# Work moved from VectorE to ScalarE and to DMA in a fused anisotropic-diffusion and ternary-convolution kernel

## The chip, the cores and the metric

One core of one Trainium2 chip runs the whole program. The metric is the device time of one execution in microseconds (us); the table below has the median of three runs. The engines are TensorE (PE, matmuls and transposes into PSUM), VectorE (DVE), ScalarE (ACT), GpSimd (POOL, here memsets and the issue of DMAs that add to their destination) and SyncE (SP, here only the issue of DMAs). Each engine runs its own instructions in order; semaphores tie them together.

## The reference

The input x is 8 x 32 x 32 x 64 (batch, row, column, channel), fp32. Cut to what matters:

```python
s = gn(x)                                   # 32 groups of 2 channels, over rows, columns and group
g, g1 = relu(bn(dwconv3x3(s, wg))), relu(bn(dwconv3x3(s, wg1)))
gy, gx = sobel(s)                           # reflecting border
Dx, Dy = 1 / (gy*gy/4 + 1), 1 / (gx*gx/4 + 1)
ux = 0.5 * (roll(g, 1, column) - roll(g, -1, column))
vy = 0.5 * (roll(g1, 1, channel) - roll(g1, -1, channel))
Bx, By, E = 0.2*Dx, 0.2*Dy, 0.2*(ux + vy)
D = 1 / (1 + 2*Bx + 2*By)
h = h0 = s
for _ in range(5):
    prev = h
    h = D * ((1 - 2*Bx - 2*By)*h0 - 2*E*h + (2*Bx - 0.2*g)*roll(h, 1, column) + (2*Bx + 0.2*g)*roll(h, -1, column)
             + (2*By - 0.2*g1)*roll(h, 1, channel) + (2*By + 0.2*g1)*roll(h, -1, channel)) + 0.4*D*s
    h0 = prev
x = x + relu(bn(h))
W3 = alpha * ternary(W)                     # 3 x 3 x 64 x 64, alpha a mean over the kept weights
return x + relu(conv3x3(gn(x), W3) + b)
```

## The kernel before

**Layout.** The batch of 8 is cut in two tiles t of four images. A tile has image row and image on the 128 partitions and 32 columns x 64 channels = 2048 fp32 numbers (1 MB in all) in each; a pass over a tile is thus 128x2048. `coef[:, t, i]` are seven such planes for each tile, `state[:, t, k]` two planes with a border, `ring` three planes. PSUM is used as four slots of 128x1024; `job_table()` gives each PE result (`gy_0_0` is Sobel y, tile 0, half 0) its slot, and PE waits until the slot's former result was read. The order on each engine is written out by hand. `wait_job` waits for a result of PE, `wait_reader` for the engine that reads it.

**First stage, both tiles.** DVE sums x by group, PE averages over partitions, DVE subtracts (`centre`), ACT squares (`square_of`), DVE sums, PE averages (`var_t`), and the inverse root is made by ACT (`rsqrt_first`: Ln, Exp) and one Newton step on DVE (`rsqrt`). `scale_grouped(t)` (L706, DVE) writes the scaled tile in the channel order that the depthwise convolution wants, `scale_s(t)` (L713, DVE) scales it in place. `split_hi` (L718) rounds it to fp32r, `split_lo` (L721) makes the remainder. PE transposes the grouped form (`t2`), applies the Sobel matrices to high and low part (`gy`, `gx`), and runs both depthwise convolutions (`cv_t_0` to `cv_t_3`, L1109 and L1114, with taps that ACT has scaled in `scale_taps`). ACT squares the Sobel results into planes 0 and 1 and brings the convolutions back (`to_natural`).

**Second stage.** `shifted(t)` adds a constant to plane 1 (DVE for tile 0, L789; ACT for tile 1), `denominator(t)` multiplies (DVE), `reciprocal_first(t)` is Ln and Exp on ACT, `newton(t)` two DVE passes. `across_rows` and `across_columns` make planes 4 and 5, `both_diffusivities(t)` (L819, DVE) their sum in plane 2. From it ACT makes D-related planes (`d_of`, `a0_of`), DVE the tap planes (`over_rows`, `over_channels`), and POOL issues DMAs that add the opposite taps (`other_rows`, `other_channels`, `first_source`). The divergence of tile 0 is made by DVE and additive DMAs, with `minus_g` from ACT; that of tile 1 by PE (`divergence`, L1145), for which all `cv_1` must have been read.

**Ring.** A step (k, t) is five or six DVE products of a coefficient plane and a shifted state (L897) into three ring planes; PE transposes and sums them in PSUM (L1155), ACT takes them out, PE turns them back (L1062). `ORDER` interleaves the tiles.

**Tail.** For each tile: `residual` adds x (DVE) and takes statistics, PE averages (`mean2_t`, `var2_t`), `spread` and `second_norm` (DVE, with `rsqrt_first` on ACT) give scale and shift, `normalise` writes eight 64x512 pieces with a step of four numbers (ACT three, DVE five), `upper_half` (ACT) and `lower_half` (DVE) split the result, PE runs the 3x3 convolution (`dense`, L1233) and ACT its ReLU (`relu_dense`), DVE adds (`output_sum`), PE turns the result (`out_natural`), ACT takes it out (`take_out`) and SP stores it. Tile 0 has two such parts, tile 1 four.

## Time and profile before

| | us |
|---|---|
| median of 3 runs | 284.3 (283.94 to 284.4) |
| the profiled execution | 284.37 |
| its span, first to last instruction | 282.6 |
| VectorE busy | 251.6 |
| TensorE busy | 235.3 |
| ScalarE busy | 130.0 |
| first ring product on VectorE starts | 92.97 |

The span is 1.8 us shorter than the time, since the start and the end of an execution lie outside it. An engine that is busy for most of the span need not be what sets the end; that is read from what each waits for. In a timeline row, the brackets behind a group say how long the engine idled ahead of it and what ended that.

### The profile page before, as it was taken

To read this page: it belongs to the slowest core of one execution; us is meant where nothing else is said; L and a number is where in the kernel's file an instruction comes from. 1 tells how busy PE (TensorE), PEld (TensorE's weight loads), DVE (VectorE), ACT (ScalarE), POOL (GpSimd) and SP (SyncE) were. 2 spreads that over 40 slices of the span, in tenths; PEclk is the share of its full clock that TensorE was granted. 3 is DMA by queue.
4 is the path that set the end of the run, shared out by engine and by line. 5 is a ranking of instruction groups with operands and counts; after the bars stand their busy time and mean duration, and the time that the engine had idled before them with its cause. 6 is when DMAs were issued, how large, how long until landed. Compare 5 with 4: busy or idle time off the path is not lost.

```text
span 282.6 us, 5201 instructions
## 1 busy us (share of the span) xinstructions
PE 235.3 (83%) x2264; PEld 210.7 (75%) x2264; DVE 251.6 (89%) x199; ACT 130.0 (46%) x202; POOL 15.9 (6%) x35
## 2 busy tenths in 40 slices
PE   0137999999759998279999999999999876699793
PEld 0136899889725597279999999898989776688682
DVE  3899999999999979999999999999999978986820
ACT  3295678876973204602723516061420515336743
POOL 2000000003300101111000101010101000000000
PEclk9999999999968999959999999999999999979999
DMA  7950000007992701990700425176700040000123
GB/s 201 345 118 0 0 6 3 2 0 148 205 207 43 148 0 37 203 204 3 151 0 2 93 58 111 39 174 125 148 3 1 0 147 3 2 0 0 45 106 148
DMA packets 6758, 22.84 MB, mean 81 GB/s; under 512 B 2768, under 2 KB 3024, under 8 KB 4944
## 3 DMA queue, kind: packets, MB, share of 16 engines
q0 software_dynamic: 2160, 13.63, 24.2%
q1 hardware_dynamic: 4432, 8.56, 9.9%
q8 instruction: 18, 0.29, 0.4%
q10 hardware_dynamic: 144, 0.33, 0.4%
q14 instruction: 4, 0.03, 0.0%
HBM read 6.79 MB, written 2.10 MB: 31 GB/s over the span
## 4 chain that ended last, share of the span: by engine, by line
DVE 49%; PE 36%; issue 8%; ACT 4%; DMA 1%; DVEq 0%; ACTq 0%
DVE ring L897 22%; PE psum L1155 16%; DVE coef L637 8%; PE psum L1233 7%; PE psum L1145 7%; PE psum L1062 3%; DVE first_two L980 3%; DVE coef L940 2%; PE psum L1092 2%; ACT coef L370 2%; DVE lo_s L721 2%; DVE state L713 2%; DVE ring L706 1%; DMA bn<-in_norms 1%; DVE hi_s L718 1%
## 5 line engine op out<-in xcount | busy, mean ns | idle before, releaser
L897 DVE TENSOR_TENSOR ring<-coef,state 128x2048 f32<-128x2048 f32 x51 | 113.4, 2286 | 2.7 <-PE psum L1155 2.5
L1155 PE MATMUL psum<-mats,ring 128*128 128x128 f32 x816 | 97.7, 280 | 13.8 <-DVE ring L897 13.8
L1155 PEld LDWEIGHTS psum<-mats,ring 128*128 128x128 f32 x816 | 92.5, 145 | 17.2 <-DVE ring L897 16.7
L370 ACT ACTIVATE state<-psum 128x1024 f32<-128x1024 f32 x36 | 35.1, 1029 | 83.9 <-PE psum L1155 70.1
L637 DVE SCALAR_TENSOR_TENSOR coef<-coef 128x2048 f32<-128x2048 f32 x16 | 36.6, 2290 | 0.5
L1114 PEld LDWEIGHTS psum<-coef,state 32*128 32x128 f32 x672 | 19.4, 187 | 1.7 <-issue 1.7
L1114 PE MATMUL psum<-coef,state 32*128 32x64 f32 x672 | 20.1, 271 | 0.2 <-issue 0.2
L1233 PE MATMUL psum<-hi,dense_m 128*128 128x512 f32 x48 | 20.0, 417 | 0.0
L370 ACT ACTIVATE coef<-psum 128x512 f32<-128x512 f32 (+1 forms) x22 | 17.3, 791 | 5.7 <-PE psum L1092 4.3
L1233 PE MATMUL psum<-lo,dense_m 128*128 128x512 f32 x48 | 19.3, 403 | 0.0
L1155 PE MATMUL psum<-mats,first_two 128*128 128x128 f32 x144 | 17.2, 273 | 1.2 <-ACT state L370 1.2
L370 ACT ACTIVATE coef<-coef 128x2048 f32<-128x2048 f32 (+1 forms) x10 | 17.6, 1779 | 0.2
L1155 PEld LDWEIGHTS psum<-mats,first_two 128*128 128x128 f32 x144 | 16.0, 141 | 1.4 <-ACT state L370 1.4
L1062 PE MATMUL psum<-mats,state 128*128 128x128 f32 x128 | 15.4, 273 | 0.7 <-ACT state L370 0.7
L1062 PEld LDWEIGHTS psum<-mats,state 128*128 128x128 f32 x128 | 14.1, 141 | 1.2 <-ACT state L370 1.1
L1145 PE MATMUL psum<-coef,mats 128*128 128x512 f32 (+2 forms) x20 | 9.8, 632 | 4.6 <-ACT first_two L370 4.6
L951 DVE TENSOR_TENSOR coef<-coef 128x512 f32<-128x512 f32 (+1 forms) x6 | 5.2, 870 | 8.3 <-ACT coef L370 8.3
L1092 PE MATMUL psum<-lo_s,sobel_m 128*128 128x512 f32 (+2 forms) x48 | 11.4, 372 | 0.5 <-DVE lo_s L721 0.5
L1092 PE MATMUL psum<-hi_s,sobel_m 128*128 128x512 f32 (+2 forms) x48 | 11.3, 372 | 0.5 <-DVE hi_s L718 0.5
L980 DVE TENSOR_TENSOR first_two<-coef,state 128x2048 f32<-128x2048 f32 x5 | 11.4, 2285 | 0.0
L1246 PE MATMUL psum<-gsum,mats 128*128 128x32 f32 x4 | 1.2, 404 | 12.1 <-DVE gsum L671 12.1
L370 ACT ACTIVATE coef<-psum,outp,wred 128x512 f32<-128x512 f32 (+1 forms) x6 | 5.5, 918 | 11.9 <-PE psum L1233 11.9
(132 smaller groups left out, 277.3 us busy)
## 6 DMA issues: line engine op xcount, KB each, us to landing
first_two<-coef POOLq DMA_DIRECT2D x7, 1024.0 KB, 7.3
coef<-coef POOLq DMA_DIRECT2D x4, 1024.0 KB, 9.0
coef<-in_x SPq DMA_DIRECT2D x2, 1024.0 KB, 7.2
coef<-in_wide_taps SPq DMA_DIRECT2D x3, 384.0 KB, 8.0
ring<-in_x SPq DMA_DIRECT2D x2, 512.0 KB, 6.1
ring<-in_x SPq DMA_DIRECT2D x1, 1024.0 KB, 11.2
out<-coef SPq DMA_DIRECT2D x2, 512.0 KB, 3.1
out<-coef SPq DMA_DIRECT2D x4, 256.0 KB, 2.4
```

Source lines behind the costliest of these rows:

```text
L370: return nc.scalar.activation(dst, src, func, **kw)
L637: return V.scalar_tensor_tensor(out=out_ap, in0=in0, scalar=scalar, in1=in1, op0=op0, op1=op1)
L713: signal(V.tensor_tensor(s, s, root(t).unsqueeze(1).broadcast_to([128, W, C]), ALU.mult), s_ready, t + 1)
L721: V.tensor_tensor(wc(s_parts[1][:, :]), h_at(t, 0), wc(s_parts[0][:, :].bitcast(f32)), ALU.subtract)\
L897: V.tensor_tensor(wc(ring[:, slot, :]), wc(coef[:, t, a, :]), h_at(t, k, dw, dc), ALU.mult)\
L980: V.tensor_tensor(wc(first_two[t][:, :]), wc(coef[:, t, A0, :]), h_at(t, k), ALU.mult)\
L1062: ins = nc.tensor.transpose(dst[:, j * 128:j * 128 + 128], src, ident)
L1092: ins = mm(dst[:, bank * BANK + to * C:bank * BANK + (to + count) * C], sobel_m[:, m, :], part[:, frm * C:(frm + count) * C], start=(i == ...
L1114: ins = mm(banks[a][:, j * 2 * W:(j + 1) * 2 * W], sT[t][p, 8 * h + j, dy * BT:dy * BT + 128], taps(8 * h + j)[p, dy, :, :].rearrange("p v ...
L1145: ins = mm(out_ap, m, src, start=(i == 0), stop=(i == len(pieces) - 1), skip_group_check=True)
L1155: ins = mm(slot_ap(name)[:, (j % 8) * 128:(j % 8) * 128 + 128], src[:, j * 128:j * 128 + 128], ident, is_transpose=True, start=first and j ...
L1233: ins = mm(to, dense_m[:, b, dy, :], rows[:, j0 + b:j0 + b + 4, dy * BT:dy * BT + 128], start=(n == 0), stop=(n == len(steps) - 1))
```

## The change

- Tile 0's rounding (`split_hi(0)`), tile 0's shifted square (`shifted(0)`) and tile 1's grouped order (`reorder(1)`, a copy of the already scaled tile in place of `scale_grouped(1)`) are made by ACT. DVE's `scale_s(1)` comes right behind its root, `split_hi(1)` and `denominator(0)` behind that. The ternary weights are made in three pieces instead of two.
- ACT scales the taps of groups 5 to 12 in one go ahead of `split_hi(0)`; `square_of(1)` comes ahead of the transposes' copies. PE runs both high passes of the y Sobel of tile 0 ahead of both low ones, and `var_1` ahead of the x Sobel.
- On ACT `d_of(0)` comes ahead of the second Sobel square of tile 1, `minus_g` behind it, and the copies into `dense_m` ahead of `reciprocal_first(1)`.
- `both_diffusivities(1)` is replaced by two DMAs: SP copies plane 4 into plane 2 once `across_rows(1)` is done, POOL adds plane 5. `d_of(1)` waits for them.
- In the tail, `group_mean2(0)` moves ahead of the source's transposes of step (4, 1), `group_var2(0)` one product forward, the asking for the root is a step of its own behind the first product, and ACT normalises six of tile 0's eight pieces. `group_mean2(1)` and `group_var2(1)` move into `dense(0, 0)`, behind matmuls 18 and 22 of 24. Tile 1's output is cut in 512, 512, 512, 256 and 256 columns instead of four times 512.

On ACT, the rows ahead of tile 0's reciprocal (`coef<-coef,minus`): the squares of the Sobel results are `coef<-psum 128x1024`. Before:

```order
L370 ACTIVATE coef<-psum 128x1024 [waits pe_job] x3
L370 ACTIVATE rs_ln<-rs_in 128x32 [waits rs_asked]
L370 ACTIVATE rs_y<-rs_ln 128x32 [waits act_step]
L370 ACTIVATE coef<-psum 128x1024 [waits pe_job]
...
L370 ACTIVATE last_taps<-last_taps,scales 128x3x32 [waits taps_in4]
L370 ACTIVATE last_taps<-last_taps,scales 128x3x32
L370 ACTIVATE coef<-coef,minus 128x2048 [waits den_const,u_ready]
```

And now, with the shift and the grouped copy between the last square and the reciprocal:

```order
L380 ACTIVATE coef<-psum 128x1024 [waits pe_job] x2
L380 ACTIVATE coef<-coef 128x2048 [waits slot_free0,slot_free3]
L380 ACTIVATE ring<-state 128x128x8x2 [waits s_ready]
L380 ACTIVATE coef<-coef,minus 128x2048 [waits den_const,u_ready]
L380 ACTIVATE coef<-coef 128x2048 [waits act_step]
```

Two full passes stand where the remaining taps stood, and the taps moved forward.

On ACT, from the copy of -g (`state<-coef`) to the first `to_natural` of tile 1; `d_of(0)` is the row that waits for sb_ready. Before:

```order
L370 ACTIVATE state<-coef 128x2048 [waits slot_free0,slot_free1,slot_free3,slot_free2]
L370 ACTIVATE coef<-psum 128x1024 [waits pe_job] x3
L370 ACTIVATE coef<-coef 128x2048 [waits sb_ready]
L370 ACTIVATE coef<-psum 128x1024 [waits pe_job]
L370 ACTIVATE coef<-coef 128x2048 [waits slot_free3,slot_free2]
L370 ACTIVATE coef<-coef 128x2048
L370 ACTIVATE coef<-coef,minus 128x2048 [waits den_const,u_ready]
```

And now:

```order
L380 ACTIVATE coef<-psum 128x1024 [waits pe_job]
L380 ACTIVATE coef<-coef 128x2048 [waits sb_ready]
L380 ACTIVATE coef<-psum 128x1024 [waits pe_job]
L380 ACTIVATE state<-coef 128x2048 [waits slot_free0,slot_free1,slot_free3,slot_free2]
L380 ACTIVATE coef<-psum 128x1024 [waits pe_job] x2
L380 ACTIVATE coef<-coef 128x2048 [waits slot_free3,slot_free2]
L380 ACTIVATE coef<-coef 128x2048
L380 ACTIVATE dense_m<-ring 64x3x64 [waits zero_ready,tern_ready]
```

`d_of(0)` moved from behind the third square to behind the first, `minus_g` from ahead of all to the middle.

On DVE, the rows from the root of tile 1 to `newton(0)` (the row that waits for y_ready). Before:

```order
L706 TENSOR_TENSOR ring<-state,gsum 128x128x8x2 [waits xm_ready,dve_step]
L789 TENSOR_SCALAR coef<-coef 128x2048 [waits slot_free0,slot_free3]
L637 SCALAR_TENSOR_TENSOR coef<-coef 128x2048 [waits shifted_ready,slot_free2,slot_free1]
L713 TENSOR_TENSOR state<-state,gsum 128x32x64 [waits s_grouped_ready,u_ready]
L718 CAST hi_s<-state 128x2048 [waits pe_job,s_ready]
L721 TENSOR_TENSOR lo_s<-state,hi_s 128x2048 [waits s_hi]
L637 SCALAR_TENSOR_TENSOR coef<-coef 128x2048 [waits y_ready]
```

And now:

```order
L747 TENSOR_TENSOR state<-state,gsum 128x32x64 [waits xm_ready,dve_step]
L751 CAST hi_s<-state 128x2048 [waits pe_job,s_ready]
L668 SCALAR_TENSOR_TENSOR coef<-coef 128x2048 [waits shifted_ready,slot_free2,slot_free1]
L755 TENSOR_TENSOR lo_s<-state,hi_s 128x2048 [waits s_hi,u_ready]
L814 TENSOR_SCALAR coef<-coef,wred 128x576
L668 SCALAR_TENSOR_TENSOR ring<-coef,wred 128x576 [waits dve_step]
L668 SCALAR_TENSOR_TENSOR coef<-coef 128x2048 [waits y_ready,tern_ready]
```

The first two rows are gone, and the denominator stands behind the scaling and the rounding of tile 1.

The diff, cut to its core:

```diff
+        act_pieces = (((1, 0), (1, 1), (1, 2), (1, 3), (0, 0), (0, 1)), ((1, 0), (1, 1), (1, 2)))
+        dve_pieces = (((0, 2), (0, 3)), ((0, 0), (0, 1), (0, 2), (0, 3), (1, 3)))
+        out_cuts = ((0, HALF, N), (0, BANK, 2 * BANK, 3 * BANK, 3 * BANK + BANK // 2, N))
...
+            sp.wait_ge(row_part, 2)
+            sp.dma_start(coef[:, 1, 2, :], coef[:, 1, 4, :]).then_inc(sb_begun, 16)
...
             other_channels(0)
+            pool.wait_ge(sb_begun, 16)
+            pool.wait_ge(column_part, 2)
+            pool.dma_start(coef[:, 1, 2, :], coef[:, 1, 5, :], accum_op=ALU.add).then_inc(sb_added, 16)
             first_source(0)
...
+            def split_hi(t):
+                act.wait_ge(s_ready, t + 1)
+                copy(wc(s_parts[0][:, :]), h_at(t, 0)).then_inc(s_hi, 1)
+            def shifted(t):
+                for h in range(2):
+                    wait_reader(act, f"gx_{t}_{h}")
+                copy(coef[:, t, 2, :], coef[:, t, 1, :], bias=(1.0 + 2 * DT) * S).then_inc(shifted_ready, 1)
+            def reorder(t):
+                act.wait_ge(s_ready, t + 1)
+                copy(s_grouped[t].rearrange("p (g a w e) -> p a w g e", e=2, a=CP, w=W),
+                     h_at(t, 0).rearrange("p w (a g e) -> p a w g e", a=CP, e=2)).then_inc(s_grouped_ready, 1)
...
-            step(STEPS - 1, 1, ((-1, lambda: spread(0)), (1, lambda: second_norm(0)), (3, lambda: normalise(0))))
+            step(STEPS - 1, 1, ((-1, lambda: spread(0)), (0, lambda: ask_norm(0)), (1, lambda: second_norm(0)),
+                                  (3, lambda: normalise(0))))
...
+                if (k, t) == ORDER[-1]:
+                    group_mean2(0)
                 take_sums(t, k)
                 add_source(t, k)
...
-            dense(0, 0)
+            dense(0, 0, 0, 18)
             group_mean2(1)
-            dense(0, 1, 0, 4)
+            dense(0, 0, 18, 22)
             group_var2(1)
-            dense(0, 1, 4)
+            dense(0, 0, 22)
+            dense(0, 1)
```

## Rows read from the trace of the kernel before

**Rows 1.** the page's busy time of each engine: us, share of the span, instructions

```profile
PE 235.3 (83%) x2264; PEld 210.7 (75%) x2264; DVE 251.6 (89%) x199; ACT 130.0 (46%) x202; POOL 15.9 (6%) x35
```

**Rows 2.** timeline of DVE, 24 to 110: start, us, line, operation, shapes, count

```profile
24.69 1.23 DVE L718 CAST hi_s<-state 128x2048 fp32r<-128x2048 f32 x1
...
37.88 2.29 DVE L706 TENSOR_TENSOR ring<-state,gsum 128x2048 f32<-128x2048 f32 x1
40.09 1.22 DVE L789 TENSOR_SCALAR coef<-coef 128x2048 f32<-128x2048 f32 x1
...
49.57 9.27 DVE L637 SCALAR_TENSOR_TENSOR coef<-coef 128x2048 f32<-128x2048 f32 x4
...
84.77 2.29 DVE L819 TENSOR_TENSOR coef<-coef 128x2048 f32<-128x2048 f32 x1
...
92.97 6.70 DVE L897 TENSOR_TENSOR ring<-coef,state 128x2048 f32<-128x2048 f32 x3
...
101.49 4.49 DVE L897 TENSOR_TENSOR ring<-coef,state 128x2048 f32<-128x2048 f32 x2 [1.82 <-PE psum L1155]
```

**Rows 3.** timeline of ACT, 37 to 83

```profile
37.48 1.02 ACT L370 ACTIVATE coef<-psum 128x1024 f32<-128x1024 f32 x1 [0.98 <-PE psum L1092]
...
43.77 2.01 ACT L370 ACTIVATE coef<-coef,minus 128x2048 f32<-128x2048 f32 x1 [2.09 <-DVE coef L637]
...
76.69 2.02 ACT L370 ACTIVATE dense_m<-ring 64x192 fp32r<-64x192 f32 x6
...
80.83 1.91 ACT L370 ACTIVATE first_two<-state 128x2048 f32<-128x2048 f32 x1
```

**Rows 4.** timeline of PE, 62 to 105

```profile
62.54 1.11 PE L1109 MATMUL psum<-shift_rows,ones_r 128*128 128x512 f32 x4
...
74.81 1.60 PE L1114 MATMUL psum<-last_taps,state 32*128 32x64 f32 x46
81.06 3.86 PE L1145 MATMUL psum<-coef,mats 128*128 128x512 f32 x6 [4.64 <-ACT first_two L370]
...
91.61 1.96 PE L1145 MATMUL psum<-coef,mats 128*128 128x512 f32 x4
...
99.44 5.44 PE L1155 MATMUL psum<-mats,ring 128*128 128x128 f32 x48
```

**Rows 5.** stretches on PE: us, busy, granted clock, DMA share, GB/s

```profile
80.00:84.00 4.00, 2.94 (x4) 0.50 1.05 199
...
244.00:248.00 4.00, 2.02 (x14) 0.88 0.00 0
```

**Rows 6.** groups of instructions on ACT, shapes apart

```profile
L370 ACT ACTIVATE coef<-coef,gn 64x512 f32<-64x512 f32 x6 | 7.4, 1308 | 1.8 <-DVE gn L637 1.8
```

**Rows 7.** the page's DMA issues: KB of each, median us to landing

```profile
coef<-coef POOLq DMA_DIRECT2D x4, 1024.0 KB, 9.0
coef<-in_x SPq DMA_DIRECT2D x2, 1024.0 KB, 7.2
```

**Rows 8.** timeline of DVE, 228 to 262

```profile
228.63 0.17 DVE L637 SCALAR_TENSOR_TENSOR spreads<-psum,stats 128x8 f32<-128x8 f32 x1 [1.94 <-PE psum L1212]
...
243.63 2.29 DVE L897 TENSOR_TENSOR ring<-coef,state 128x2048 f32<-128x2048 f32 x1
...
255.54 0.17 DVE L637 SCALAR_TENSOR_TENSOR spreads<-psum,stats 128x8 f32<-128x8 f32 x1 [2.20 <-PE psum L1212]
...
258.45 3.45 DVE L940 TENSOR_SCALAR coef<-coef,gn 64x512 f32<-64x512 f32 x5
```

**Rows 9.** timelines of PE and of ACT, 237 to 280

```profile
237.89 1.97 PE L1155 MATMUL psum<-mats,ring 128*128 128x128 f32 x16 [2.06 <-DVE ring L897]
...
245.98 2.71 PE L1155 MATMUL psum<-mats,ring 128*128 128x128 f32 x16 [2.17 <-DVE ring L897]
...
255.26 1.21 ACT L370 ACTIVATE coef<-psum,outp,wred 128x1024 f32<-128x1024 f32 x1 [5.32 <-PE psum L1233]
...
279.11 0.60 ACT L370 ACTIVATE coef<-psum 128x512 f32<-128x512 f32 x1 [0.50 <-PE psum L1062]
```

More of the change, by code:

```diff
@@ L552, in relu_dense @@
                 wait_job(act, name)
[L553 removed]
+                frees(copy(part(coef[:, t, 0, :], t, h), part_slot(name, t, h), ACT.Relu, scale=wred[:, 7:8],
                            bias=outp[:, 4:5]), name)
@@ L609, in _ @@
             relu_dense(1, 3)
-            for q in range(1, 4):
-                take_out(1, q)
+            take_out(1, 1)
+            relu_dense(1, 4)
+            for i in range(2, 5):
+                take_out(1, i)
         @blk.vector
@@ L1041, in _ @@
             output_sum(0, 1)
-            for q in range(4):
-                output_sum(1, q)
+            for i in range(5):
+                output_sum(1, i)
         @blk.tensor
@@ L1314, in _ @@
             dense(1, 3)
-            for q in range(1, 4):
-                out_natural(1, q)
+            out_natural(1, 1)
+            dense(1, 4)
+            for i in range(2, 5):
+                out_natural(1, i)
     return nc
```

159 lines of the change are left out of this document (83 added, 76 removed), and 2 rows, old and new, of the table early.

## The prediction

> **What bounds the kernel now.** Read first the page's busy line: VectorE (DVE) is busy for 89% of the span, TensorE (PE) for 83%, ScalarE (ACT) for 46% [rows 1]. So work taken from DVE should pay, but PE runs almost as densely. Next the timelines, to see which wait stands where. Up to the first ring product at 92.97 DVE hardly waits; the first wait that counts is 1.82 us ahead of 101.49, and it is for PE [rows 2]. PE's timeline says why: it ends the divergence of tile 1 only at 99.44, and it began that at 81.06 after 4.64 us of idleness, waiting for ACT [rows 4]. So two paths meet at 101.49: DVE's own passes, and PE's chain depthwise(1), to_natural(1) on ACT, divergence. From there to 224 DVE has next to no idle time, so what is won at 101.49 is kept, and the ring steps, unchanged, are not costed. The third place is the tail: DVE waits 1.94 and 2.20 us for the two group means [rows 8].
>
> **The front, DVE and ACT up to newton(0).** Four whole passes leave DVE: the rounding of tile 0 (1.23), the grouped scaling of tile 1 (2.29), the shift of tile 0 (1.22), the sum of the diffusivities of tile 1 (2.29) [rows 2]: 7.0 us. They are not all gained. Times below are on the clock of before.
> - split_hi(0) on ACT starts with the scaled state at 24.65 and takes a plain pass, 1.91 [rows 3]: 26.6, against 25.9 before. PE's Sobel work starts 0.6 later, but without the wait for the low half behind it, so depthwise(0) starts where it did, at 37.2. The taps that ACT now scales ahead of it lie in time in which it waited. var_1 comes two microseconds earlier, so scale_s(1) is over at 37.6.
> - Then ACT is late. The last square of tile 0 cannot start before PE is done: 37.5 before [rows 3], 37.3 by my sum. Square 1.02 to 38.3, shifted(0) 1.9 to 40.2, and only then denominator(0) on DVE, 2.3 to 42.6; DVE waits some 1.35 us there. The reciprocal on ACT is 2.01 + 1.91 [rows 3]: y is there at 46.6. split_lo(1) and the ternary sign hide under it. newton(0) begins at 46.6 instead of 49.57 [rows 2]: 3.0 gained, of 4.7 removed so far.
> - reorder(1) has room for 2.4 us on ACT between 40.2 and 42.6 before it delays that reciprocal. Its cost isn't in the trace. Ends: a plain pass, 1.91 [rows 3], and four times the 64x512 piece that steps 16 bytes on both sides, 4 x 1.31 = 5.2 [rows 6]. It reads runs of 16 numbers and writes them in pairs. DVE made the very same pattern in 2.29, as long as its contiguous sum (2.29) [rows 2], so I take 1.9, hidden; the other end is a rival.
>
> The Trainium skill, SBUF — State Buffer, section "Door 1: The DMA port swizzle", says that SBUF has 16-byte lines and that two hits in a line are needed for the full rate. Pairs of fp32 give two hits, the 16-byte step only one; by that rule reorder(1) is 1.9 and the normalising pieces are the slow ones, which is how the two rows stand. The sum doesn't need it.
>
> **From newton(0) to the first products.** Four passes 9.3 and the sum 2.3 [rows 2] give sb(0) at 58.2. ACT's order is new here, and every item of it stands ahead of something. It reaches d_of(0) at 56.6 and waits for 58.2. Then d_of(0) 1.8, square (1,0,1) 1.0, minus_g 1.8, square (1,1,0) 1.0: 63.85. PE's depthwise(1) needs the bank of that last square; it began at 62.54 [rows 4] and now at 63.85, a new wait of 1.3. Square and shifted(1): 66.75, where DVE, there at 65.6, has waited 1.1 for denominator(1). a0_of(0) 1.8, the copies to dense_m 2.02 [rows 3], which are new ahead of the reciprocal: 70.5. Reciprocal 3.9: 74.4. newton(1) starts at 74.45 (75.6 before), and from there DVE has 4.65 + 2.25 + 2.25 without the sum of 2.3, then divergence_added 2.3, source(0) and small ones 3.8: first product at 89.65, against 92.97 [rows 2]. DVE gains 3.3 here.
> PE: depthwise(1) takes 13.87 (62.54 to 76.41) [rows 4], so 77.7. to_natural's last four pieces follow at once, since dense_m is out of the way: about 2.05 to 79.8; the divergence starts at 80.05 (81.06). PE has then idled 2.3, not 4.64. After the 4.64 it ran at half clock, 0.50 granted at 80 to 84 [rows 5], and the first half of the divergence took 10.55 where the second, the same 26 matmuls, took 7.83 [rows 4]: 2.7 lost. Without the fall the whole is 15.7 and ends at 95.7. With 2.17 us of idle time ahead of 245.98 the clock did fall (0.88, and sixteen transposes took 2.71); after 2.06 ahead of 237.89 they took 1.97 as ever [rows 5, 9]. 2.3 lies beside these. I take no fall, and 1.7 as the price of a shorter one. So PE starts the products at 95.7, DVE's fourth product at 97.8 instead of 101.49: **3.7 gained**, with DVE still waiting 1.4 for PE. That wait means DVE's path has slack left; PE decides.
>
> **The sum made by DMA.** The rows' part is done at 81.4. No copy inside SBUF is in the trace: the nearest rows are the load of 1 MB, 7.2, and the addition of 1 MB, 9.0 [rows 7]: 88.6 to 90.4. POOL then issues the addition (0.9) and it takes 7.2 to 9.0: sb_added at 96.7 to 100.3; d_of(1) 1.9: 98.6 to 102.2. over_rows(1) wants it at 102.2. It fits, with nothing to spare at the far end; I take the middle, 98.5, as two other additions share the engines for part of it. Behind the waiting POOL stands first_source(0), wanted by its data at 88.3 and issued at 90.1, behind the addition in the same queue: by the same rows 98 to 104. PE wants it at 101.0. Lateness of up to 3 us lands in PE's idle time before 121.96, not in DVE's path. Nothing else of POOL or SP is pending there.
>
> **The tail.** group_mean2(0) moved ahead of the source transposes: the 1.94 wait goes (halo_ready then allows DVE at 227.0, and spread(0) is over at 227.4, against 229.3). group_var2(0) is one product earlier on PE, and ask_norm(0) waits for it about 0.8; three of five pieces of DVE's normalise(0) leave: 3 x 0.69 = 2.1. The last product ends at 242.0 instead of 243.6 + 2.3 = 245.9 [rows 8]. ACT has six pieces for three, at most 1.31 each [rows 6] and 7.5 as they overlap, from 233.85: 241.4, then the upper half to 243.5; lower_half(0) on DVE thus ends at 245.1 against 248.3, and residual(1) at 250.05 against 253.35 (255.54 less its wait): 3.3. PE stands behind matmul 18 of dense(0,0) by 248.4 and waits for the statistics, so the mean is made at once: the 2.20 wait [rows 8] shrinks to 0.6. But relu_dense(0,0) (1.21) [rows 9] is ahead of rsqrt_first on ACT, and its data now come after group_var2(1), with the last two matmuls, at 252.45. So the root is given at 254.1, not at 252.6: 1.5 of the 5.1 is handed back. normalise(1) starts at 254.95 against 258.45 [rows 8]: 3.5. Behind it PE's 48 matmuls are the same. Cutting the last quarter in two puts four transposes (0.4) ahead of the end and halves what follows the last matmul, 0.78 + 0.69 + 0.60 of ACT, DVE, ACT (the last in [rows 9]) and the store: some 0.8. Net 0.4. **Tail: 3.9.**
>
> **Sum.** The profiled execution took 284.37 (span 282.6); less 3.7 and 3.9: 276.8. The median of the three runs, 284.3, is 0.07 lower, so 276.7.
>
> **Rivals.**
> - **The clock falls** in the shorter idle time ahead of the divergence. The 2.17 us row speaks for it, the 2.06 us one against. PE ends 1.7 to 2.7 later: 278.4 to 279.4. The skill's TensorE: Matmul & The Clock Gate, "Part 1", makes the clock depend on activity in windows that run free of the kernel; by that the same idle time can go either way, which the two rows allow. Chance 0.25.
> - **reorder(1) is slow**, 5.2. It ends at 45.4, newton(0) starts at 49.3, d_of(0) and with it depthwise(1) slip by 2.7 (PE idles 4.0, long enough for the fall seen after 4.64), the divergence ends at 98.4 to 101.1. Front gain 1.0 to -1.7: 279.5 to 282.2. Against it: DVE's row of the pattern. Chance 0.1.
> - **The tail gives less**, because ACT's six pieces and not DVE gate the lower half, or the wait of PE inside dense(0,0) drops its clock (as at 248, 1.6 lost): 278.4. Chance 0.15.
> - **The DMA sum decides, and the kernel is slower.** d_of(1) is the only way to over_rows(1). If copy, issue and addition together take longer than 18.9 us from 81.4, each further microsecond is DVE's; to be slower than before they must eat 7.6 + 0.6 us, 27 in all, which is half as long again as the worst of the rows (9.0 + 0.9 + 9.0 [rows 7]). That gives 285. Halfway there, 23 us, it is 281. For it: a copy from SBUF to SBUF loads the same memory twice, and the queue also carries other_channels(0). Chance 0.1 for a late sum, 0.03 of it for slower.
>
> **How the numbers follow.** The forecast itself (no fall, fast pattern, DMA in time) has 0.4, 276.7 with its own range 275 to 278. The clock and the thin tail add 0.4 up to 279.4. The slow pattern and the late DMA reach 282; half of these is left out: 274.8 to 280.8. A measurement of this kernel tells 0.2% (0.6 us) from no change. Only the two last rivals come near 284: faster 0.93, same 0.03, slower 0.04.
>
> **What would show it.** In the changed trace: DVE waits 1.35 for shifted(0) ahead of denominator(0); newton(0) at 46.6; the grouped copy of 1.9 on ACT; PE idle 1.3 ahead of depthwise(1) and 2.3 ahead of the divergence, at a granted clock of 1.00; DVE waiting for PE ahead of its fourth product at 97.8; d_of(1) before 102; normalise(1) 7.2 earlier than before. I am wrong if over_rows(1) waits for ACT, if the ACT copy exceeds 2.4, or if PE isn't what the fourth product waits for.

## The result, and the profile after

The changed kernel takes 287.0 us (median of 8 runs, 284.97 to 290.11) against 284.02 (8 runs, 283.53 to 284.4) of the kernel before on the same chip: a ratio of 1.0093, 95% interval 1.005 to 1.0137. It is slower, by 0.9%; 276.7 with a range of 274.8 to 280.8 was predicted. The ratios here and below compare means, and leave out an execution more than 1.5% above the fastest of its kernel (here that of 290.11, in a2 that of 288.75). The profiled execution took 285.05 (span 283.3, mean granted clock 0.961; before 282.6 and 0.967). The eight executions are of two kinds by their mean granted clock: five of 284.97 to 287.03 at 0.956 to 0.961, three of 288.61 to 290.11 at 0.937 to 0.940. What sets the second kind apart is taken up below, under b8 and d4.

The page's busy line answers to [rows 1]: VectorE has lost 9.1 us of work, ScalarE has gained 9.4, and the time went up all the same.

```profile
PE 236.8 (84%) x2276; PEld 212.6 (75%) x2276; DVE 242.5 (86%) x193; ACT 139.4 (49%) x210; POOL 16.8 (6%) x36
```

VectorE's timeline (start, us, line, operation, shapes, count, and in brackets the idle time ahead and its releaser) answers to [rows 2]:

```profile
40.48 2.29 DVE L668 SCALAR_TENSOR_TENSOR coef<-coef 128x2048 f32<-128x2048 f32 x1 [1.76 <-ACT coef L380]
...
46.86 9.15 DVE L668 SCALAR_TENSOR_TENSOR coef<-coef 128x2048 f32<-128x2048 f32 x4 [0.47 <-ACT coef L380]
...
66.95 2.29 DVE L668 SCALAR_TENSOR_TENSOR coef<-coef 128x2048 f32<-128x2048 f32 x1 [1.18 <-ACT coef L380]
...
74.54 7.01 DVE L668 SCALAR_TENSOR_TENSOR coef<-coef 128x2048 f32<-128x2048 f32 x3 [0.64 <-ACT coef L380]
83.43 2.29 DVE L668 SCALAR_TENSOR_TENSOR coef<-coef 128x2048 f32<-128x2048 f32 x1 [1.88 <-PE psum L1153]
...
91.51 6.70 DVE L931 TENSOR_TENSOR ring<-coef,state 128x2048 f32<-128x2048 f32 x3
105.65 4.50 DVE L931 TENSOR_TENSOR ring<-coef,state 128x2048 f32<-128x2048 f32 x2 [7.45 <-PE psum L1194]
```

Up to 74.54 all came as worked out, within some 0.4 us. Then VectorE waits for PE at 83.43, and for 7.45 us ahead of the fourth product, which starts at 105.65 instead of the predicted 97.8 (101.49 before). PE's timeline answers to [rows 4]; L1153 is the depthwise product, L1184 the divergence, L1194 the products' transposes:

```profile
64.15 1.10 PE L1148 MATMUL psum<-shift_rows,ones_r 128*128 128x512 f32 x4 [1.63 <-ACT coef L380]
65.19 5.34 PE L1153 MATMUL psum<-coef,state 32*128 32x64 f32 x178
70.75 0.67 PE L1153 MATMUL psum<-coef,state 32*128 32x64 f32 x14 [0.22 <-issue]
...
72.40 3.34 PE L1153 MATMUL psum<-coef,state 32*128 32x64 f32 x108
78.43 2.19 PE L1153 MATMUL psum<-coef,state 32*128 32x64 f32 x34 [2.68 <-issue]
...
80.42 2.97 PE L1153 MATMUL psum<-last_taps,state 32*128 32x64 f32 x46
85.36 3.86 PE L1184 MATMUL psum<-coef,mats 128*128 128x512 f32 x6 [1.97 <-ACT first_two L380]
89.01 3.06 PE L1184 MATMUL psum<-first_two,mats 128*128 128x504 f32 x8
...
103.60 5.44 PE L1194 MATMUL psum<-mats,ring 128*128 128x128 f32 x48
```

depthwise(1) starts at 64.15 (predicted 63.85), but inside it PE stops for 2.68 us with "issue" as releaser, that is, with no semaphore to wait for. Behind the stop it runs at half clock: the 46 last taps take 2.97 where they took 1.60 [rows 4]. The stretches (us, PE, weight loads, VectorE, ScalarE, GpSimd busy, granted clock, DMA share, GB/s) show the clock falling in that stop:

```profile
72.00:76.00 4.00, 3.74 (x111) 3.27 (x109) 3.36 (x2) 3.97 (x6) 0.86 (x1) 1.00 1.04 206
76.00:80.00 4.00, 1.57 (x32) 1.57 (x32) 3.86 (x3) 0.45 (x1) 0.00 (x0) 0.62 1.07 202
80.00:84.00 4.00, 3.39 (x60) 3.20 (x58) 2.12 (x2) 0.96 (x2) 0.00 (x0) 0.50 0.99 227
```

The 7.9 us between 97.8 and 105.65 are, nearly all: 0.3 of later start; 2.7 of stop; some 2.3 of half clock in what follows of the depthwise product (34 matmuls 2.19 against 1.22, 46 last taps 2.97 against 1.60); 2.5 of half clock in the divergence, 18.2 (85.36 to 103.60) against the 15.7 assumed without a fall. That is 7.8.

From there nothing new happens until the tail. VectorE's product of step (4, 1) starts at 228.57; before it was 224.41, and the difference, 4.16, is that of the fourth product (105.65 less 101.49).

### The profile page after: what moved, and what is told of

Same layout as the page of the kernel before. It is cut to its first block, busy times and chain, and to the rows that moved or that the text cites. A ratio compares the mean times of both kernels' runs of the same rounds, so it can differ in the third digit from the quotient of the medians.

```text
span 283.3 us, 5236 instructions
## 1 busy us (share of the span) xinstructions
PE 236.8 (84%) x2276; PEld 212.6 (75%) x2276; DVE 242.5 (86%) x193; ACT 139.4 (49%) x210; POOL 16.8 (6%) x36
## 4 chain that ended last, share of the span: by engine, by line
DVE 42%; PE 41%; issue 8%; ACT 7%; DMA 1%; DVEq 0%; ACTq 0%
DVE ring L931 21%; PE psum L1194 16%; PE psum L1184 6%; DVE coef L668 6%; PE psum L1153 5%; PE psum L1271 5%; ACT coef L380 4%; PE psum L1099 4%; PE psum L1130 4%; DVE first_two L1017 3%; DVE coef L977 2%; DMA bn<-in_norms 1%; ACT state L380 1%; DVE gsum L702 1%; DVE state L714 1%
## 5 line engine op out<-in xcount | busy, mean ns | idle before, releaser
L1194 PE MATMUL psum<-mats,ring 128*128 128x128 f32 x816 | 96.9, 278 | 10.2 <-DVE ring L931 10.1
L1194 PEld LDWEIGHTS psum<-mats,ring 128*128 128x128 f32 x816 | 91.9, 144 | 13.6 <-DVE ring L931 13.2
L1153 PEld LDWEIGHTS psum<-coef,state 32*128 32x128 f32 x672 | 20.7, 194 | 4.5 <-issue 4.5
L1153 PE MATMUL psum<-coef,state 32*128 32x64 f32 x672 | 21.6, 280 | 2.9 <-issue 2.9
L380 ACT ACTIVATE coef<-coef 128x2048 f32<-128x2048 f32 (+1 forms) x11 | 19.5, 1793 | 9.0 <-DMA coef<-coef 6.8
L380 ACT ACTIVATE coef<-psum 128x512 f32<-128x512 f32 (+2 forms) x23 | 17.3, 761 | 10.6 <-PE psum L1153 7.7
L1271 PE MATMUL psum<-hi,dense_m 128*128 128x512 f32 (+1 forms) x54 | 20.0, 379 | 0.9 <-ACT coef L380 0.9
L1271 PE MATMUL psum<-lo,dense_m 128*128 128x512 f32 (+1 forms) x54 | 19.5, 368 | 0.0
L1194 PE MATMUL psum<-mats,first_two 128*128 128x128 f32 x144 | 17.2, 273 | 1.2 <-issue 1.2
L1194 PEld LDWEIGHTS psum<-mats,first_two 128*128 128x128 f32 x144 | 16.0, 141 | 1.4 <-ACT state L380 1.4
L380 ACT ACTIVATE coef<-coef,gn 64x512 f32<-64x512 f32 x9 | 11.3, 1319 | 3.4 <-DVE gn L668 3.4
L988 DVE TENSOR_TENSOR coef<-coef 128x512 f32<-128x512 f32 (+2 forms) x7 | 5.4, 768 | 8.2 <-ACT coef L380 8.1
L380 ACT ACTIVATE coef<-psum,outp,wred 128x512 f32<-128x512 f32 (+2 forms) x7 | 5.9, 838 | 13.0 <-PE psum L1271 13.0
L1271 PEld LDWEIGHTS psum<-hi,dense_m 128*128 128x128 f32 x54 | 10.2, 188 | 2.7 <-issue 1.1
L1184 PE MATMUL psum<-coef,mats 128*128 128x512 f32 (+2 forms) x20 | 9.8, 632 | 2.0 <-ACT first_two L380 2.0
```

Source lines behind the costliest of these rows:

```text
L380: return nc.scalar.activation(dst, src, func, **kw)
L988: V.tensor_tensor(part(coef[:, t, 3, :], t, h), part(coef[:, t, 0, :], t, h), part(coef[:, t, 2, :], t, h), ALU.add).then_inc(sum_ready, 1)
L1153: ins = mm(banks[a][:, j * 2 * W:(j + 1) * 2 * W], sT[t][p, 8 * h + j, dy * BT:dy * BT + 128], taps(8 * h + j)[p, dy, :, :].rearrange("p v ...
L1184: ins = mm(out_ap, m, src, start=(i == 0), stop=(i == len(pieces) - 1), skip_group_check=True)
L1194: ins = mm(slot_ap(name)[:, (j % 8) * 128:(j % 8) * 128 + 128], src[:, j * 128:j * 128 + 128], ident, is_transpose=True, start=first and j ...
L1271: ins = mm(to, dense_m[:, b, dy, :], rows[:, j0 + b:j1 + b, dy * BT:dy * BT + 128], start=(n == 0), stop=(n == len(steps) - 1))
```

## The experiments

Each is compared with runs of the kernel before on the same chip; the chips differ between some of the experiments, so times of two experiments are compared with some care. Where a diff says "after", it starts from the changed kernel.

**The tail alone** (a1_tail_only): the kernel before with the tail's part of the change: the jobs `mean2`, `var2` and the last quarter's in their new places, `ask_norm(0)`, six pieces for ScalarE, the last output cut in two.

> The kernel before with the changes of the tail alone (group means placed earlier, ask_norm, six of tile 0's eight pieces on ScalarE, five output parts). Theory 1: the tail's gain is its own and does not depend on the front: 3.4 to 3.9 us less than before, 280.4 to 280.9, normalise(1) about 3.4 earlier than in the kernel before. Rival: the tail only caught up on a delay that the front brought in; alone it gives under 1 us: 283.2 or more.

Measured 279.85 (279.72 to 279.92), ratio 0.9854 (0.9817 to 0.9891), 4.2 us below the kernel before and a little better than expected. Not all of it is the tail. In this profile the fourth product starts at 100.52, against 101.49 [rows 2]:

```profile
100.52 4.49 DVE L904 TENSOR_TENSOR ring<-coef,state 128x2048 f32<-128x2048 f32 x2 [0.77 <-PE psum L1167]
```

These 0.97 us come from the divergence, which no edit touched: PE's second group of it (8 matmuls) took 2.25 here and 3.20 before, as the granted clock rose sooner after the idle time (0.93 against 0.67 in 84 to 88). normalise(1) starts at 254.07, 4.38 earlier than before, and 3.4 of that arise in the tail. So the tail is worth about 3.5 of the 4.5 us by which the spans differ (282.6 and 278.1), the rest is luck with the clock, and the other parts of the change cost some 6 to 7 us.

**Small additions** (a2_small_adds): after, with the three large additions of tile 0 cut to 64 columns of 2048; a part of tile 0's coefficients is thus left out.

```diff
-                pool.dma_start(coef[:, t, AXM, :], coef[:, t, AXP, :], accum_op=ALU.add)
+                n = N if t else C
+                pool.dma_start(coef[:, t, AXM, 0:n], coef[:, t, AXP, 0:n], accum_op=ALU.add)
```

(and the same for AYM, and for -g)

> The changed kernel, with three DMA additions of tile 0 (taps by rows, taps by channels, the large one of -g) cut from 2048 or 1984 columns to 64; their sums are left out for the other columns, so the output is another. All waits stay. Theory 1 (TensorE's stop of 2.68 us inside depthwise(1) is its own instruction block, which comes by DMA and stands behind the packets of these additions): no stop of over 0.5 us there, granted clock 1.00 through depthwise(1), the fourth product at 96 to 98.5, time 277 to 279. Rival 2 (the stop belongs to the place in TensorE's program, or to its late start at 64.15): the stop stays at 2 us or more, fourth product at 104 to 106, time 285.

Measured 280.23 (278.96, 279.25, 281.22, 288.75), ratio 0.9863 (0.979 to 0.9937); the median of the first three is 279.25. The stop is gone, the second half of the depthwise product runs in one piece at full clock, and the divergence starts 4.9 us sooner:

```profile
72.50 4.25 PE L1155 MATMUL psum<-coef,state 32*128 32x64 f32 x144
...
80.44 3.71 PE L1186 MATMUL psum<-coef,mats 128*128 128x512 f32 x6 [2.35 <-ACT first_two L382]
```

The engines' work is untouched by this edit, only the DMAs moved less. So the stop comes from DMA traffic. The one execution of 288.75 had a mean clock of 0.941, the others 0.982: this suggests that the clock can fall without the stop, too.

This run also tests the prediction's "I take no fall". The idle time ahead of the divergence is 2.35 us here, the 2.3 that was forecast, and the clock did fall:

```profile
80.00:84.00 4.00, 3.56 (x7) 0.57 0.31 119
```

The divergence took 17.3 us (80.44 to 97.77) instead of 15.7, and the fourth product started at 99.82, not at the 96 to 98.5 expected. So even without the stop the forecast would have been some 2 us short (1.7 of it this fall).

**The old order on ScalarE** (a3_act_order): after, with the order of before around tile 1's squares.

```diff
-            sobel_square(1, 0, 0)
-            d_of(0)
-            sobel_square(1, 0, 1)
             for q in range(4):
                 wait_reader(act, f"cv_0_{q}")
             copy(minus_g, gN[0], scale=-1.0).then_inc(minus_ready, 1)
+            sobel_square(1, 0, 0)
+            sobel_square(1, 0, 1)
             sobel_square(1, 1, 0)
+            d_of(0)
             sobel_square(1, 1, 1)
```

> The changed kernel with ScalarE's order around the Sobel squares of tile 1 as in the kernel before (minus_g ahead of all squares, d_of(0) behind the third). depthwise(1) starts at 62.4 instead of 64.15, d_of(0) ends at 63.2. Theory 1: TensorE asks for its next instruction block at 68.7, when the additions have just been issued, as in the kernel before; the stop is under 0.6, the fourth product at 96.5 to 98.5 and the time 277 to 279. Rival 2: the additions are now some 3 us earlier than in the kernel before, so the block still stands behind them: stop of 1 to 2.5, the clock falls, time 281 to 284. Rival 3: d_of(0) 1.3 us later makes VectorE late and it decides: fourth product not waiting for TensorE.

Measured 286.34 (285.83 to 287.42), ratio 1.0103 (1.0067 to 1.014). Theory 1 is a miss. The second rival had the stop and the fall right, but its 281 to 284 was still too low. depthwise(1) did start without a wait, at 62.26, but the stop only moved to the first half, and from there the whole second half ran at half clock (7.96 for the 144 matmuls that took 4.25 above):

```profile
70.75 1.12 PE L1153 MATMUL psum<-coef,state 32*128 32x64 f32 x14 [2.10 <-issue]
...
73.80 7.96 PE L1153 MATMUL psum<-coef,state 32*128 32x64 f32 x144
```

Which border of PE's program meets the traffic is a matter of when PE gets there. The wait for `d_of` was not the cause.

**The root first** (a4_order_root): a3 with ScalarE giving the root of tile 1 ahead of the ReLU.

```diff
-            relu_dense(0, 0)
             rsqrt_first(128, BT)
+            relu_dense(0, 0)
             normalise(1)
```

> As the run with the old order of squares, and in the tail the root of tile 1 (rsqrt_first) ahead of relu_dense(0, 0) on ScalarE. VectorE waited 1.92 for the root in the changed kernel. Theory 1: this wait falls to 0.6 and the time is 1.3 to 1.6 below that of the run with the old order alone. Rival: relu_dense(0, 0), now behind the root, makes output_sum(0, 0) or the free slot late, and under 0.5 is gained.

Measured 285.43 (284.44 to 286.78), ratio 1.006 (1.0031 to 1.0088): 0.9 below a3, less than the 1.3 to 1.6 expected. The wait for the root itself shrank by 1.5, from 1.92 to 0.39.

**A plain transfer, and an adding one.** b5_plain_load is the kernel before with 1 MB more of plain DMA, b6_more_adding the kernel before with 1 MB more of additive DMA, each at about the time of depthwise(1); both write to an output that is overwritten later. The addition needs something to add to, so b6 also copies the same 1 MB there by a plain transfer at 18.5 us, far ahead of the place in question.

```diff
+            sp.wait_ge(sb_ready, 1)
+            sp.dma_start(out_nat[0], x_nat[0]).then_inc(extra_in, 16)
```

```diff
+            pool.wait_ge(sb_ready, 1)
+            pool.dma_start(out_nat[0], x_nat[0], accum_op=ALU.add).then_inc(extra_added, 16)
             pool.wait_ge(e_made, 3)
```

> The kernel before with one more transfer that nothing needs: SyncE copies 1 MB of the input to the output's place in HBM when the first sum of diffusivities is ready (61.2 us); the stores at the end overwrite it. Theory 1a (any transfer in flight holds TensorE's instruction block back): the block that is fetched at 65.1 in the kernel before comes at 68 or later, TensorE stops for 1.5 to 2.5 us with no cause shown near 68.7, again near 73.5, and the time is 2 to 5 us longer. Theory 1b (only the additions issued by GpSimd do so): the block still comes at 65 to 66, no new stop of over 0.5, time within 1 us of before.

> The kernel before with the same useless 1 MB, but as an addition that GpSimd issues at 61.2 us ahead of its others (input added to the output's place, overwritten at the end). Theory 1, either form: the block fetched at 65.1 comes when this addition is over, 67 to 69; a stop of 1 to 2.5 us near 68.7 and one near 73.5, granted clock 0.50 behind them, and 3 to 7 us more in all. Rival 2 (TensorE's stops belong to its program and its late start): no stop of over 0.5, within 1.5 us of before.

Measured: the plain transfer 284.06 (282.13 to 284.85), ratio 0.9975 (0.9948 to 1.0002); the addition 289.56 (287.54 to 290.29), ratio 1.0178 (1.0134 to 1.0221). PE with the plain one, then with the added one:

```profile
63.48 5.59 PE L1118 MATMUL psum<-coef,state 32*128 32x64 f32 x192
...
70.06 4.36 PE L1118 MATMUL psum<-coef,state 32*128 32x64 f32 x142
```

```profile
71.39 1.13 PE L1120 MATMUL psum<-coef,state 32*128 32x64 f32 x14 [2.48 <-issue]
...
74.45 7.96 PE L1120 MATMUL psum<-coef,state 32*128 32x64 f32 x144
```

One useless addition by DMA gives the kernel before a stop and a fall like those of the changed kernel and of a3, though one stop where two were expected. The same size of plain traffic does nothing: it was in flight from 61.1 to 66.3. The two transfers differ in two things, since the plain one was issued by SyncE on another queue and the addition by GpSimd. A plain transfer issued by GpSimd was not tried, so whether the adding or GpSimd's queue counts stays open.

**Whose wait it is.** One of the profile's DMA queues is named "instruction": q8, with 18 packets of 16 KB in the run. (A second of that name, q14, has only four small packets, none of them between 60 and 110 us.) The 2276 matmuls of the run are 126 for each packet of q8, and 126 is also the number of matmuls between the two stops of the changed kernel (14, 4 and 108). Narrow windows of the DMA view date its packets to 0.1 us. For after at 76.1 to 76.2:

```profile
q8 instruction: 1, 0.02, 59.1%
```

| kernel | packets of q8 while depthwise(1) runs, us | PE's stops with releaser "issue" |
|---|---|---|
| before | 65.0, 71.3, 79.0 | 0.25, to 73.75 |
| after | 68.4, 76.1, 83.3 | 0.22, to 70.75; 2.68, to 78.43 |
| a2_small_adds | 68.4, 72.3, 76.1 | 0.22, to 70.84 |
| a3_act_order | 68.2, 75.5, 83.1 | 2.10, to 70.75 |
| b5_plain_load | 65.7, 70.8, 77.1 | none |
| b6_more_adding | 69.0, 75.3, 81.1 | 2.48, to 71.39 |
| c1_split_adds | 68.4, 73.5, 77.1 | none |

Each stop ends 2.3 to 2.6 us behind a packet (76.1 and 78.43; 68.4 and 70.75; 68.2 and 70.75 in a3; 69.0 and 71.39; in before 71.3 and 73.75). The reading that fits all of them is that PE had run out of instructions and resumed when the next block was in.

What a packet waited for can be read as well. The first large addition of the changed kernel was issued at 61.2 and landed after 7.0 us, at 68.2:

```profile
ring<-coef POOLq DMA_DIRECT2D x1, 992.0 KB, 7.0
```

The packet came at 68.4. In the same way landing and packet stand at 71.1 and 71.3 in before, 68.3 and 68.4 in a2, 68.0 and 68.2 in a3, 71.0 and 70.8 in b5, 68.1 and 68.3 in b8, and in c1, where that addition was cut in halves, at 68.5 and 68.4, then 73.4 and 73.5. For the later additions it is less neat: in after the packet of 76.1 comes 1.4 us behind the landing of the rows' addition (65.7 and 9.0), in before that of 79.0 likewise (68.5 and 9.1), and b6's packets fit no landing as closely. The Trainium skill, Runtime: NRT & Kernel Launch, section "Instruction fetch mechanics", says that each engine's sequencer fetches its program in blocks of 16 KiB by a DMA queue of its own and that crossing a border is mostly hidden. The packets of 16 KB agree; "hidden" doesn't hold here, with 2.1 to 2.7 us of stop where additive DMAs were in flight. In before it was all but hidden: 0.25 us with the same releaser ahead of 73.75, a row that I had passed over:

```profile
73.75 1.22 PE L1114 MATMUL psum<-coef,state 32*128 32x64 f32 x34 [0.25 <-issue]
```

**The sum on VectorE** (b7_sum_on_vector): after, without the copy and the addition that make tile 1's sum; VectorE makes it as before.

```diff
             across_columns(1)
+            both_diffusivities(1)
             divergence_added()
```

> The changed kernel with the sum of tile 1's diffusivities on VectorE again, and neither the copy by SyncE nor the addition by GpSimd. Theory 1: VectorE waits 7.45 us for TensorE ahead of the fourth product, so 2.3 more on VectorE change nothing: within 0.6 us of the changed kernel, the stop inside depthwise(1) stays, since both transfers were issued after it. Rival: the transfers delayed something else (first_source(0) landed 11.2 us after its issue), and without them the time falls by 1 us or more.

Measured 286.09 (284.91 to 290.21), ratio 1.0082 (1.0045 to 1.0119), against 1.0093 of the changed kernel. The DMA-made sum gains nothing and costs nothing measurable, since VectorE waits for PE at that place with or without it.

**The additions held back** (b8_held_adds): after, with the additions of -g issued only when PE is well into depthwise(1) (`cv_1_1` done), and the rows' and channels' behind them.

```diff
-            other_rows(0)
             pool.wait_ge(e_some, 32)
             pool.wait_ge(minus_ready, 1)
+            wait_job(pool, "cv_1_1")
```

> The changed kernel, with GpSimd's order for tile 0 altered: the two additions of -g wait until TensorE has done the first half of depthwise(1) (71.4), and the taps' additions by rows and by channels come behind them. All sums are made. Theory 1: when TensorE asks for its block at 70.75 nothing is in flight, so no stop of over 0.3 us in depthwise(1) apart from the 0.22 at 70.7; fourth product at 97.8 to 100, time 277.5 to 279.5. Rival 2: the stop of 2 to 2.7 us stays, and 285 with it. Rival 4: the additions, now late, hold divergence_added or the third and fourth product up: VectorE waits for a DMA.

Measured 288.59: one execution of 281.22 with a mean clock of 0.984, three of 288.57 to 290.43 with 0.937. So the time is a miss, and even the best execution is 1.7 above the range expected. No stop remains in the profile, which is of one of the three (288.6). Its PE rows and four of the stretches:

```profile
64.14 1.10 PE L1149 MATMUL psum<-shift_rows,ones_r 128*128 128x512 f32 x4 [1.62 <-ACT coef L381]
65.17 9.70 PE L1154 MATMUL psum<-coef,state 32*128 32x64 f32 x192
...
76.81 7.96 PE L1154 MATMUL psum<-coef,state 32*128 32x64 f32 x144
```

```profile
64.00:68.00 4.00, 3.86 (x72) 3.50 (x76) 2.72 (x5) 3.91 (x3) 0.00 (x0) 0.77 0.99 184
68.00:72.00 4.00, 4.00 (x84) 4.00 (x83) 3.93 (x3) 3.90 (x8) 0.00 (x0) 0.50 0.02 5
...
80.00:84.00 4.00, 4.00 (x84) 4.00 (x80) 1.54 (x1) 0.00 (x0) 0.00 (x0) 0.50 1.08 202
...
92.00:96.00 4.00, 4.00 (x13) 2.17 (x12) 3.67 (x8) 0.41 (x2) 0.93 (x2) 0.82 0.67 152
```

Here the clock fell behind the 1.62 us of idle time ahead of depthwise(1), and it stayed at 0.50 (1.2 of 2.4 GHz) for the whole of the product, although PE was busy without a gap from 68 to 84. It rose at 92 to 96, in the divergence. So there is a second mechanism: a fall ahead of the depthwise product costs all of it. This is probably also the second kind of execution of the changed kernel, and that of a2's 288.75: their mean clocks, 0.937 to 0.941, are those of this profile, and all three kernels have the idle time of 1.6 us there. No profile of such an execution of those two was taken, so this rests on the clock and the time.

**The order alone** (d4_order_alone): the kernel before with ScalarE's new order around tile 1's squares (the reverse of a3's diff), nothing else. It makes the idle time ahead of depthwise(1) long.

> The kernel before with one part of the change alone: ScalarE's new order around tile 1's squares (depthwise(0)'s difference behind the first square, the scaled copy behind the second), so that depthwise(1) gets its data later. Nothing else is changed. Theory (an idle of TensorE ahead of depthwise(1) makes the clock fall, and the depthwise product does not bring it back): the idle ahead of depthwise(1) is 3 to 5 us, the granted clock is about 0.50 through the whole of depthwise(1), its second half's 144 matmuls take 7.96 instead of 4.25, and the fourth product starts at 108 or later: about 290. Rival (the clock comes back within depthwise(1), so that only the later start counts): at most 288, with the second half at 4.25.

Measured 296.72 (295.33 to 298.02), ratio 1.0473 (1.0415 to 1.0532). The theory holds, with a fall in all four executions by their mean clocks (0.917 to 0.928), and it had underrated the price, about 290 (the first half counts as well):

```profile
67.03 2.05 PE L1109 MATMUL psum<-shift_rows,ones_r 128*128 128x512 f32 x4 [4.30 <-ACT coef L370]
69.00 10.52 PE L1114 MATMUL psum<-coef,state 32*128 32x64 f32 x192
...
81.46 7.96 PE L1114 MATMUL psum<-coef,state 32*128 32x64 f32 x144
...
113.70 4.49 DVE L897 TENSOR_TENSOR ring<-coef,state 128x2048 f32<-128x2048 f32 x2 [4.34 <-PE psum L1155]
```

```profile
84.00:88.00 4.00, 4.00 (x84) 0.50 0.58 117
```

There is no "issue" wait in these rows, so this is the fall without the stop. The 4.5 us of later start cost 12.2 us at the fourth product (101.49 to 113.70). A part of the change that was there to let `d_of(0)` go earlier is by itself the worst of all edits tried.

**Both mended** (c1_split_adds): after with a3's order and a4's root, and the additions spread out: -g's partner in two halves, one behind the other, and rows and channels behind -g.

```diff
-            pool.dma_start(e0[:, C:N], gN[0][:, 0:N - C], accum_op=ALU.add).then_inc(e_some, 16)
+            pool.dma_start(e0[:, C:HALF], gN[0][:, 0:HALF - C], accum_op=ALU.add).then_inc(e_some, 16)
+            pool.wait_ge(e_some, 16)
+            pool.dma_start(e0[:, HALF:N], gN[0][:, HALF - C:N - C], accum_op=ALU.add).then_inc(e_some, 16)
```

> The changed kernel with three edits: ScalarE's old order around tile 1's Sobel squares (no wait of TensorE ahead of depthwise(1)), the root ahead of relu_dense(0, 0), and GpSimd's first addition for tile 0 split in two halves, the second issued when the first has landed, the additions by rows and channels behind those of -g. Theory 1 (a block of TensorE's instructions waits for the additions already in flight, and the clock, once fallen, stays at half through depthwise(1)): the first half is over at 65.6, so the block asked for at 64.8 comes at 65.6 to 66, the next at 70 to 71; no stop of over 0.6 us in depthwise(1), granted clock 1.00 from 62 to 76, the fourth product at 97 to 98.5, and the time 274 to 276.5 in every execution. Rival 2: the block waits for all additions of the kernel that GpSimd has queued, or the stops are the program's: a stop of 2 us stays, time 284 or more, as with the old order alone.

Measured 279.03 (278.09 to 280.78), ratio 0.9843 (0.9798 to 0.9887). Stop and half clock in depthwise(1) are gone in this profile (its second half took 4.30), as meant; the size was missed, 279.03 against at most 276.5. But the profile doesn't show the case that was meant: depthwise(1) started at 65.24, not at 62.4, and its packet came at 68.4, not by 66. Whether the other executions have a stop isn't shown; their mean clocks, 0.975 to 0.979, speak against a long fall. The profiled execution, the slowest of the six, shows two reasons for the miss, one at each end of this part:

```profile
27.58 5.19 PE L1132 MATMUL psum<-hi_s,sobel_m 128*128 128x512 f32 x14 [0.90 <-ACT hi_s L382]
...
109.49 2.80 PE L1196 MATMUL psum<-mats,first_two 128*128 128x128 f32 x16 [4.22 <-DMA first_two<-coef]
```

The first 14 Sobel matmuls of tile 0 took 5.19 instead of 3.21, with a granted clock of 1.00 on record. In the next kernel the same rows took 5.38, and its six executions fall in two groups 2.0 us apart. And `first_source` was late for PE: GpSimd issued it at 98.0, as it had waited until then for the copy of tile 1's sum, which took 11.8 us to land behind the additions that had been moved back.

**With the sum back on VectorE** (c3_split_vsum): c1 without the copy and the addition of tile 1's sum.

> c1_split_adds with one thing changed: VectorE makes tile 1's sum itself (as in the kernel before), so neither the copy nor the addition of tile 1's sum is sent by DMA. Theory (the copy and the addition delay first_source of ring 1, whose data TensorE waited 4.22 us for in c1): the wait for first_source goes to under 2, VectorE pays about 0.5 to 2.3 us for the sum, the time is 276.5 to 278. Rival (VectorE decides there and the DMA wait was covered by it): 279 or more, the wait gone and VectorE's products later by the sum's duration.

Measured 278.78 (277.74 to 280.27), ratio 0.9832 (0.9789 to 0.9875); three executions at 277.74 to 277.78, three at 279.78 to 280.27. The wait for `first_source` is gone, as the theory has it, and VectorE runs through its fourth product (from 95.05 five products in 11.10, no wait). The faster group is in the expected range, the median just above it, and the slower group is where the rival had put it. Its sign is there as well: VectorE's first product starts at 95.05 against 93.31 in c1, though the fifth ends no later.

**The tail with the root first** (c2_tail_root): a1 with a4's edit.

> The kernel before with the tail's changes and the root ahead of relu_dense(0, 0). Theory 1: the front of the kernel before is untouched (blocks at 65.1 and 71.3), and the root gives 1.3 to 1.6 us on top of the tail's 4.1: 278.2 to 278.6. Rival: under 0.5 on top, 279.4 or more.

Measured 278.95 (278.64 to 279.58), ratio 0.9839 (0.9798 to 0.988), 0.9 below a1 and just above the expected 278.2 to 278.6. VectorE's wait for the root in a1, then here:

```profile
253.28 0.16 DVE L661 TENSOR_TENSOR rs_t<-rs_y 128x4 f32<-128x4 f32 x1 [1.92 <-ACT rs_y L374]
```

```profile
251.68 0.16 DVE L661 TENSOR_TENSOR rs_t<-rs_y 128x4 f32<-128x4 f32 x1 [0.38 <-ACT rs_y L374]
```

It gained 1.54 at the root and kept 0.9 (medians, on two chips) to 1.3 (spans 278.1 and 276.8) of it. This is the kernel to keep: 8 us under the changed one, and with a spread of 0.9 us. c3 is level with it for all the work it moves.

## Why the prediction was wrong, point by point

**The front up to 74.5: right.** DVE's wait for the shifted square 1.76 (1.35 predicted), `newton(0)` at 46.86 (46.6), depthwise(1) at 64.15 behind 1.63 of idle time (63.85, 1.3), `newton(1)` at 74.54 (74.45). The grouped copy on ScalarE, its cost unknown ahead, was at the low end taken. It is the second row here:

```profile
38.44 1.91 ACT L380 ACTIVATE coef<-coef 128x2048 f32<-128x2048 f32 x1
40.26 2.08 ACT L380 ACTIVATE ring<-state 128x2048 f32<-128x2048 f32 x1
42.81 2.00 ACT L380 ACTIVATE coef<-coef,minus 128x2048 f32<-128x2048 f32 x1 [0.47 <-DVE coef L668]
```

So the rival of a slow pattern falls. The Trainium skill's rule on 16-byte lines (SBUF — State Buffer, "Door 1: The DMA port swizzle") agrees: the pass in pairs took 2.08, a plain one 1.91.

**"PE: depthwise(1) takes 13.87, so 77.7": the step that failed.** It took 19.2 (64.15 to 83.39; ScalarE's `to_natural` pieces waited until 83.04). The duration was carried over from a profile in which the same additive DMAs stood elsewhere against PE's program. The change sends the first addition and the rows' 2.8 us earlier (61.2 and 65.7, against 64.0 and 68.5) and starts depthwise(1) 1.6 us later, so two large additions are in flight when PE comes to the end of a block of instructions. a2, b5 and b6 show from three sides that the stop hangs on the additions; that it is the block that comes late is read from q8's packets. The sum had costed each DMA by whether its own data came in time, and never by what else waits for the DMA system.

**"I take no fall": wrong as well, and the rival was priced for one place only.** It was priced at 1.7 to 2.7 us for a fall ahead of the divergence. That fall comes even without the stop: a2 had the forecast 2.35 us of idle time there, and lost 1.7. In the trace of the changed kernel the clock fell earlier, in the stop, and cost 2.3 and 2.5 us; in other executions it seems to have fallen ahead of depthwise(1), where b8 and d4 show that the product doesn't bring it back: 192 and 144 matmuls take 9.70 and 7.96 instead of 5.59 and 4.25, 7.8 us more, and the divergence's share comes on top. The new idle time of 1.3 us ahead of depthwise(1) was forecast correctly and given no chance to lower the clock. By the mean clocks it did so in three of eight executions.

**"PE starts the products at 95.7, 3.7 gained": 103.60, 4.2 lost.** That VectorE would wait for PE there, and that PE decides, was right; the wait is 7.45 instead of 1.4.

**The DMA-made sum: in time, worth nothing.** The copy landed after 6.4 us, POOL's addition after 7.0, `d_of(1)` was over at 97.2, and VectorE came to `over_rows(1)` at 110.06. The rival in which it decides falls. b7 shows that without it the time is the same: the 2.3 us that it takes off VectorE lie in front of a wait for PE.

**The tail: right, 3.5 instead of 3.9,** here and in a1's profile, once the 0.97 us that a1 won ahead of the tail is taken off. VectorE's rows answer to [rows 8], ScalarE's six pieces are the last row:

```profile
230.76 0.16 DVE L668 SCALAR_TENSOR_TENSOR spreads<-psum,stats 128x8 f32<-128x8 f32 x1
...
234.53 0.16 DVE L961 TENSOR_SCALAR rs_in<-psum 128x4 f32<-128x4 f32 x1 [0.81 <-PE psum L1256]
...
246.74 2.50 DVE L983 TENSOR_TENSOR lo<-coef,hi 128x1152 fp32r<-128x1152 f32 x2 [0.74 <-ACT hi L380]
...
258.43 0.16 DVE L685 TENSOR_TENSOR rs_t<-rs_y 128x4 f32<-128x4 f32 x1 [1.92 <-ACT rs_y L380]
...
259.22 3.46 DVE L977 TENSOR_SCALAR coef<-coef,gn 64x512 f32<-64x512 f32 x5
```

```profile
237.72 7.65 ACT L380 ACTIVATE coef<-coef,gn 64x512 f32<-64x512 f32 x6 [2.55 <-DVE gn L668]
```

The wait for the mean is gone and 0.81 is left for the variance, both as worked out; ScalarE's six pieces gate the lower half, the rival's case, but by 0.74 only. normalise(1) starts at 259.22, 3.4 sooner than before on the shifted clock (258.45 and 4.16), with 3.5 predicted; the root handed back by the ReLU is the row of 1.92. Only the cut of the last quarter gave next to nothing, 0.1 instead of 0.4: a piece of 256 columns took ScalarE 0.57 and VectorE 0.42, not half of 0.78 and 0.69.

**One slip in the chances.** "Only the two last rivals come near 284" doesn't fit the list: the thin tail stands at 278.4, and the rival that comes near beside the late DMA is the slow pattern, at up to 282.2. Nothing in the sum hangs on it.

## What to carry to other kernels

A duration from the profile of before holds only while what shares the chip with it stands where it stood: when a change moves large GpSimd-issued additions against TensorE's stream, look for "issue" waits of a few tenths on TensorE first, since they mark the borders of its program where the margin is gone. Order work so that TensorE never idles ahead of many small matmuls, because in b8, d4, a3 and b6 a fall of the clock there lasted through all of them; ahead of the divergence's large matmuls it cost 1.7 to 2.7 us. And price a moved order by itself: what a new order costs (12.9 us in d4) can lie hidden under what another part of the change gives.
